# The attention's first left operand: its sums and lower parts made by VectorE instead of GpSimd, in a fused cross-attention kernel

## What is computed

```
memory_proj = jnp.einsum('bme,de->bmd', memory, W_mem)
scores = jnp.einsum('bnd,bmd->bnm', hidden_states, memory_proj) / jnp.sqrt(jnp.float32(D))
attn = jax.nn.softmax(scores, axis=-1)
memory_context = jnp.einsum('bnm,bmd->bnd', attn, memory_proj)
gate_input = jnp.concatenate([hidden_states, memory_context], axis=-1)
gate = jax.nn.sigmoid(jnp.einsum('bnf,df->bnd', gate_input, W_gate) + b_gate)
fused = hidden_states + gate * memory_context
return _rmsnorm(fused, norm_w)
```

## Time and profile before

| | us |
|---|---|
| median of 3 runs | 1519.31 |
| lowest and highest | 1518.62 and 1519.43 |
| the profiled execution | 1519.42 |
| its span, first to last instruction | 1517.6 |
| TensorE busy | 1487.8 (98%) |
| VectorE busy | 1178.0 (78%) |
| ScalarE busy | 660.8 (44%) |
| GpSimd busy | 303.0 (20%) |

### The profile page before, as it was taken

The page is one execution under the profiler, slowest core; times in us unless marked ns, Lnnn a source line. Parts: engine busy times, 40 slices in busy tenths (PEclk is TensorE's granted clock), DMA queues, the critical chain, the costliest instruction groups (busy, mean ns, idle before and its releaser), DMA issues.

```text
span 1517.6 us, 20134 instructions
## 1 busy us (share of the span) xinstructions
PE 1487.8 (98%) x6528; PEld 1225.4 (81%) x6528; DVE 1178.0 (78%) x1552; ACT 660.8 (44%) x1025; POOL 303.0 (20%) x262
## 2 busy tenths in 40 slices
PE   8999999999999989999999999999999999999997
PEld 6888888888888867888788887888788788888885
DVE  6555758777777888886778766886678989999997
ACT  4333332222222267434664277436653454444443
POOL 0000000000000394116432273208421011111111
PEclk9999999999999999999999999999999999999999
DMA  9999536333332368983699349962888545455452
GB/s 187 220 232 231 132 93 165 107 109 111 111 111 97 111 168 240 237 187 95 204 250 209 95 155 255 219 164 97 236 243 180 161 172 193 192 192 193 190 195 113
DMA packets 231181, 259.81 MB, mean 171 GB/s; under 512 B 34768, under 2 KB 178128, under 8 KB 230864
## 3 DMA queue, kind: packets, MB, share of 16 engines
q1 hardware_dynamic: 231120, 259.06, 61.4%
HBM read 170.92 MB, written 85.98 MB: 169 GB/s over the span
## 4 chain that ended last, share of the span: by engine, by line
PE 89%; DVE 3%; POOL 2%; DMA 2%; ACT 1%; SPq 1%; issue 1%; DVEq 0%; POOLq 0%; ACTq 0%
PE banks L1944 36%; PE banks L2117 19%; PE banks L1991 19%; PE banks L2037 15%; DMA region_f<-in_ctx 2%; POOL region_l L795 1%; SPq L535 0%; DVE neg_max L1551 0%; POOL region_f L775 0%; POOL region_f L785 0%; POOL region_f L784 0%; DVE region_n L390 0%; ACT region_t L1013 0%; ACT region_n L1013 0%; SPq L347 0%
## 5 line engine op out<-in xcount | busy, mean ns | idle before, releaser
L1944 PE MATMUL banks<-region_t,region_n 128*128 128x512 f32 x960 | 220.4, 392 | 7.6 <-DVE region_n L390 7.2
L1944 PEld LDWEIGHTS banks<-region_t,region_n 128*128 128x128 f32 x960 | 181.8, 190 | 45.8 <-DVE region_t L390 7.9
L775 POOL TENSOR_TENSOR region_f<-region_f 128x1024 f32<-128x1024 f32 x22 | 58.0, 2645 | 713.0 <-DVE region_f L1510 621.2
L390 DVE TENSOR_TENSOR region_t<-region_f,region_t 128x1024 fp32r<-128x1024 f32 (+2 forms) x95 | 141.3, 1505 | 69.3 <-ACT region_t L874 57.3
L1944 PE MATMUL banks<-region_n,region_l 128*128 128x512 f32 x768 | 174.7, 389 | 0.0
L1944 PE MATMUL banks<-region_t,region_l 128*128 128x512 f32 x768 | 174.7, 389 | 0.0
L1944 PEld LDWEIGHTS banks<-region_t,region_l 128*128 128x128 f32 x768 | 144.2, 188 | 29.9
L1944 PEld LDWEIGHTS banks<-region_n,region_l 128*128 128x128 f32 x768 | 144.2, 188 | 29.9
L1077 ACT CAST region_l<-banks 128x512 fp32r<-128x512 f32 x128 | 75.0, 586 | 171.4 <-PE banks L1944 85.6
L1991 PE MATMUL banks<-region_t,region_l 128*128 128x512 f32 x576 | 135.8, 389 | 0.0
L1991 PEld LDWEIGHTS banks<-region_t,region_l 128*128 128x128 f32 x576 | 108.1, 188 | 22.4
(11 more groups left out here) (126 smaller groups left out, 2390.7 us busy)
## 6 DMA issues: line engine op xcount, KB each, us to landing
region_f<-in_ctx SPq DMA_DIRECT2D x128, 256.0 KB, 5.6
region_f<-prob_scratch SPq DMA_DIRECT2D x160, 128.0 KB, 5.0
region_f<-in_x SPq DMA_DIRECT2D x64, 256.0 KB, 5.5
region_f<-in_x SPq DMA_DIRECT2D x128, 128.0 KB, 2.8
prob_scratch<-prob SPq DMA_DIRECT2D x32, 512.0 KB, 4.5
prob_scratch<-region_f SPq DMA_DIRECT2D x32, 512.0 KB, 4.8
region_f<-in_x SPq DMA_DIRECT2D x16, 1024.0 KB, 4.9
out<-region_f SPq DMA_DIRECT2D x31, 512.0 KB, 2.7
```

The source lines that it names most:

```text
L390: return nc.vector.tensor_tensor(dst, src, hi.bitcast(F32), ALU.subtract)
L775: nc.gpsimd.tensor_tensor(dst, a, b, ALU.subtract).then_inc(mt_sum, 1)
L1944: mm = nc.tensor.matmul(dst, lhs(a), rhs(b), start=first and n == 0, stop=last and n == len(PASSES) - 1)
```

## The change

Four edits, and nothing of the arithmetic.

1. GpSimd no longer forms the sums of operand 0 nor its three remainders. After the two weight sums it waits until VectorE's four sums are there, forms the sums of operand 1, and waits for operand 0's last remainder before its first remainder of operand 1 (the semaphores count all operands in order).
2. VectorE forms these sums in the place where it made weight remainders 3 and 4 (`first_q_sums`), and the remainders of operand 0 (`first_q_lo`) between and behind the last evictions. Weight remainders 3 and 4 move behind the last eviction, the third weight sum one eviction later, and the fourth weight sum behind five remainders.
3. ScalarE makes upper parts 1 and 2 of operand 0 before the third weight block, group 3 before the fifth.
4. ScalarE's upper part of the seventh weight block moves from before `seed_b` of pair 0 to behind its `keep_22`.

```
-            q_sums(0)
-            q_lo(0, 1, 2)
-            q_lo(0, 3)
+            pool.wait_ge(uq_sum, 4)
             for b in range(NB):
                 H, L = 2 * b, LPB * b
                 if b == 0:
                     q_sums(1)
+                    pool.wait_ge(uq_ready, 3)
                     q_lo(1, 1, 2, 3)
...
-            w_hi_of(0, 1, 2, 3, 4)
-            q_hi(0, 1, 2, 3)
-            w_hi_of(0, 5, 6, 7)
+            w_hi_of(0, 1, 2)
+            q_hi(0, 1, 2)
+            w_hi_of(0, 3, 4)
+            q_hi(0, 3)
+            w_hi_of(0, 5, 6)
...
                         if k == 0:
+                            if n == 0:
+                                w_hi_of(0, 7)
                             q_hi(L + 1, *((1,), (2, 3))[n])
...
+            def first_q_sums():
...
+                dve.wait_ge(uq_loaded[0], 16)
+                nc.vector.tensor_tensor(s1, a21, a22, ALU.add).then_inc(uq_sum, 1)
+                nc.vector.tensor_tensor(s3, a11, a21, ALU.subtract).then_inc(uq_sum, 1)
+                dve.wait_ge(uq_sum, 1)
+                nc.vector.tensor_tensor(s2, s1, a11, ALU.subtract).then_inc(uq_sum, 1)
+                dve.wait_ge(uq_sum, 3)
+                nc.vector.tensor_tensor(s4, a12, s2, ALU.subtract).then_inc(uq_sum, 1)
+
+            def first_q_lo(n):
+                dve.wait_ge(uq_hi, n)
+                v = left_group(0, n)
+                minus_hi(v[:, LO], q_group(0, n), v[:, HI]).then_inc(uq_ready, 1)
...
                 if i == 3:
-                    w_lo(0, 3, 4)
+                    first_q_sums()
                 if i == 4:
-                    w_sums(0, 3, 4)
+                    first_q_lo(1)
+                if i == 5:
+                    first_q_lo(2)
+                    w_sums(0, 3)
                 if i == 6:
-                    w_lo(0, 5, 6, 7)
+                    w_lo(0, 3, 4, 5, 6)
+                    first_q_lo(3)
+                    w_sums(0, 4)
+                    w_lo(0, 7)
```

More of the change, by code:

```diff
@@ L1781, in block_first @@
                     w_transpose(0, 0, (1,))
+            def first_q_sums():
+                raw, sums = q_area(0)
+                a11, a12, a21, a22 = (raw[:, CB * k:CB * (k + 1)] for k in range(4))
+                s1, s3, s2, s4 = (sums[:, CB * k:CB * (k + 1)] for k in range(4))
+                dve.wait_ge(uq_loaded[0], 16)
[9 more added lines that the diff above has]
+                minus_hi(v[:, LO], q_group(0, n), v[:, HI]).then_inc(uq_ready, 1)
             def memory_first(i):
```

## The result

The changed kernel took 1523.8 us (median of 6 runs, 1522.6 to 1524.9), before 1519.0 in the same comparison (6 runs, 1517.4 to 1519.5): a ratio of 1.0032, 95% interval 1.0021 to 1.0042. It is slower by 4.9 us. The forecast was +3.0, its range to 1525.0: the time is inside the range, but above the band that the forecast itself was given (+1.5 to +4), in that of rival B (over +4). The profiled execution took 1524.82 us, its span 1523.0.

The account below looks back on a forecast made before the run. TensorE was taken as the bound, so only its idle stretches pay: -2.8 (entry) + 3.85 (what pays for it) + 1.95 (late loads beyond that) = +3.0 on 1519.3, giving 1522.3 us; range 1518.8 to 1525.0.

Parts of the forecast that it names:

- the band that the forecast itself was given: Whole kernel: the forecast's own case, +1.5 to +4 us over before, chance 0.50.
- rival B: Second half's raw loads: land later still, at 557.1; TensorE loses 5 to 6 us, 1524.9 in all; chance 0.17.
- a load that had no term: SP's queue, load of operand 2: named as going out 5.8 us late, but given no cost in the sum.

Follow-up runs that it names:

- gpsimd_waits: Changed kernel, but GpSimd forms operand 1's sums only after VectorE has made all three remainders of operand 0; 1522.52 us, ratio 1.0024.

## What to carry to other kernels

When work is moved behind an instruction that frees a buffer, list every queue entry behind the wait for that buffer, and cost each one: here the place of a load that had no term, the second of three behind one wait, was worth 2 to 3 of the 5 us lost. VectorE and GpSimd lost time here wherever the two met on SBUF operands; setting GpSimd's work back took 2.2 us off VectorE's list and left 0.7 at the next pair. A pause of TensorE of the length seen here may cost more than it shows, so read the granted clock in 1 us stretches before an unexplained slow group is put down to a missing wait.

## What the runs showed of the hardware

- **Half clock after a pause.** In these traces the clock fell to 0.50 after idle stretches of TensorE of 1.82, 1.97, 1.98, 2.10, 2.18, 2.22, 2.33, 2.52, 2.76, 2.79, 2.81 and 2.82 us, and each time 1.5 to 1.7 us of work were lost. Between 530 and 1500 us it did not fall after others of 1.94, 2.02, 2.03, 2.06 and 2.22 us, nor after any of 1.72 or less. The drop began between 0.3 us before and 1.6 us after the end of the pause. What decides between two stretches of the same length stays open.
- **The price of the turns.** VectorE's four remainders of 128x1024 took 6.25 us against GpSimd's sums and 4.62 alone (gpsimd_waits), one of 128x256 took 0.94 and 0.41. GpSimd's sums of 128x256 took 1.56 to 1.72 us there and 0.73 to 0.76 where VectorE had no such operation (changed kernel, 552.84 to 555.8).
- **Landing times under a full queue.** In the changed kernel the four transfers of the second raw load, issued from 544.6 behind four others and operand 2's, landed 8.7 to 9.5 us after their issues, which took up to 1.8 us each. The first four took at most 0.5 us to issue and landed after 3.2 to 6.8 us.
